# Two input transfers and half a weight transfer, moved to later points of the start

## The reference

```
h    = layernorm(x)                                # per token, over 256 features
x    = x + (gelu_tanh(h @ ctx.T) * (h @ ctx.T)) @ ctx       # ctx: 120 x 256, its own for each batch
h    = layernorm(x)
h    = silu((h @ w1.T) * s1) * ((h @ w2.T) * s2)   # 256 -> 1024, twice
h    = gelu((h @ h1.T) * sh1)                      # 1024 -> 1024
h    = gelu((h @ h2.T) * sh2)                      # 1024 -> 1024
out  = x + (h @ w3.T) * s3                         # 1024 -> 256
```

## Time and profile before

| | us |
|---|---|
| median of 3 executions | 321.84 |
| lowest, highest | 321.80, 322.73 |
| the profiled execution, its own time | 321.71 |
| its span, first to last instruction | 319.9 |
| TensorE busy | 314.5 |
| VectorE busy | 264.6 |
| ScalarE busy | 221.3 |
| GpSimd busy | 58.9 |

### The profile page before, as it was taken

One profiled execution on the slowest core, in us unless ns is written; L12 is line 12 of the kernel. 1 busy time (PEld: TensorE's weight loads), 2 busy tenths in 40 slices (PEclk: granted clock), 3 DMA queues, 4 the chain that ended last, 5 costly groups with the idle time before them and its releaser, 6 DMA issues.

```text
span 319.9 us, 4926 instructions
## 1 busy us (share of the span) xinstructions
PE 314.5 (98%) x1624; PEld 227.1 (71%) x1624; DVE 264.6 (83%) x500; ACT 221.3 (69%) x372; POOL 58.9 (18%) x97
## 2 busy tenths in 40 slices
PE   8899999999999999999999999999999999999996
PEld 5799768775757666577898866886575757666695
DVE  4776996898997899998789585399899998998585
ACT  3657857683887867769924564978678976868760
POOL 4456010411120114114020003000131110201000
PEclk9999999999999999999999999999999999999999
DMA  6799999899999989997518054446699979796003
GB/s 207 252 185 270 207 262 315 320 364 398 316 338 418 310 322 219 340 291 179 154 38 292 3 193 154 180 131 232 228 256 245 420 219 370 152 245 197 2 2 137
DMA packets 31612, 74.89 MB, mean 234 GB/s; under 512 B 2144, under 2 KB 14176, under 8 KB 29024
## 3 DMA queue, kind: packets, MB, share of 16 engines
q0 software_dynamic: 21840, 52.43, 58.3%
q1 hardware_dynamic: 9744, 22.11, 20.4%
HBM read 71.39 MB, written 6.29 MB: 243 GB/s over the span
## 4 chain that ended last, share of the span: by engine, by line
PE 98%; DVE 0%; ACT 0%; issue 0%
PE P L1417 32%; PE P L1411 30%; PE P L1369 19%; PE P L1503 5%; PE P L1490 4%; PE P L1341 2%; PE P L1333 2%; PE P L1322 2%; PE P L1512 1%; PE P L1566 0%; PE P L1579 0%; PE P L1586 0%; PE P L1572 0%; DVE SLY L1172 0%; DVE hh L935 0%
## 5 line engine op out<-in xcount | busy, mean ns | idle before, releaser
L1417 PE MATMUL P<-TL,WR 128*128 128x512 f32 x448 | 107.3, 396 | 0.0
L1411 PE MATMUL P<-TH,WB 128*128 128x512 f16 x448 | 99.8, 379 | 0.0
L1417 PEld LDWEIGHTS P<-TL,WR 128*128 128x128 f32 x448 | 84.0, 188 | 18.5
L671 ACT ACTIVATE TH<-H 128x512 f16<-128x512 f32 x112 | 67.9, 625 | 22.8 <-DVE H L984 14.0
L1411 PEld LDWEIGHTS P<-TH,WB 128*128 128x128 bf16 x448 | 42.4, 98 | 53.1 <-issue 4.5
L991 DVE TENSOR_TENSOR TL<-H,TH 128x512 fp32r<-128x512 f32 x112 | 73.4, 687 | 7.0 <-ACT TH L671 4.5
L1369 PE MATMUL P<-X,W 128*128 128x512 f32 (+1 forms) x320 | 62.4, 351 | 0.0
L1369 PEld LDWEIGHTS P<-X,W 128*128 128x128 f32 x320 | 51.7, 189 | 7.9 <-issue 0.4
L984 DVE TENSOR_TENSOR H<-H 128x512 f32<-128x512 f32 x64 | 41.9, 685 | 0.0
L962 DVE SCALAR_TENSOR_TENSOR H<-P,sc,SLY 128x512 f32<-128x512 f32 (+1 forms) x40 | 25.4, 639 | 18.3 <-PE P L1369 11.0
L692 ACT ACTIVATE H<-P 128x512 f32<-128x512 f32 x48 | 28.5, 593 | 13.7 <-DMA blocks_h<-H 5.4
(11 more groups left out here) (93 smaller groups left out, 255.9 us busy)
## 6 DMA issues: line engine op xcount, KB each, us to landing
WR<-blocks_h POOLq DMA_DIRECT2D x16, 1024.0 KB, 6.9
WR<-in_h POOLq DMA_DIRECT2D x11, 1024.0 KB, 9.0
WB<-blocks_h POOLq DMA_DIRECT2D x16, 512.0 KB, 6.0
WB<-in_h POOLq DMA_DIRECT2D x12, 512.0 KB, 7.5
H<-in_h POOLq DMA_DIRECT2D x8, 512.0 KB, 15.2
blocks_h<-H SPq DMA_DIRECT2D x4, 1024.0 KB, 8.6
SLY<-in_h SPq DMA_DIRECT2D x8, 512.0 KB, 5.6
SLY<-in_w SPq DMA_DIRECT2D x6, 512.0 KB, 7.8
```

The source lines that it names most:

```text
L671: eng.activation(TH[:, f % RING, :], operand(c, L, s, kk), ACT.Copy).then_inc(s_hi, 1)
L1411: return eng.matmul(bank(c, L, s, m)[:, :], WB[r % WRING][:, at:at + 128], TH[:, fill(c, L, s, kk) % RING, :], start=(not lower_first and ...
L1417: return eng.matmul(bank(c, L, s, m)[:, :], WR[r % WRING][:, at:at + 128], TL[:, fill(c, L, s, kk) % RING, :], start=(lower_first and s in ...
```

## The change

On SyncE the scales `sc` are now issued ahead of the first wait. The third batch's input is issued behind the wait for the first half of `W12`, the fourth's behind the wait for the second half, with the context of batches 2 and 3 behind it. On GpSimd the second half of `W12` is issued behind a new wait, for the gate of the second batch.

```diff
             eng.dma_start(ct[:, 0, 1, :], ctx_tok[:, 1, :]).then_inc(s_ct[0], 16)
+            eng.dma_start(sc[:, :], cols).then_inc(s_sc, 16)
+
+            eng.wait_ge(s_w12[0], 16)
             load_x(2)
-            eng.dma_start(sc[:, :], cols).then_inc(s_sc, 16)
-
-            eng.wait_ge(s_w12[0], 16)
+            eng.wait_ge(s_w12[1], 16)
             load_x(3)
-            eng.wait_ge(s_w12[1], 16)
             load_cf(1)
             load_ct(1)
@@ gpsimd
             rstd_half(1, 0)
             rstd_half(1, 1)
+
+            eng.wait_ge(s_h, 2)
             load_w12(1)
             rstd(1, 1)
             load_upper_block(0, h1, BLOCK[0])
```

More of the change, by code:

```diff
@@ L400, in _ @@
             eng.dma_start(ct[:, 0, 1, :], ctx_tok[:, 1, :]).then_inc(s_ct[0], 16)
-            load_x(2)
             eng.dma_start(sc[:, :], cols).then_inc(s_sc, 16)
             eng.wait_ge(s_w12[0], 16)
+            load_x(2)
+            eng.wait_ge(s_w12[1], 16)
             load_x(3)
-            eng.wait_ge(s_w12[1], 16)
             load_cf(1)
```

## The result

The changed kernel takes 324.06 us (median of 10, 323.60 to 326.25) against 321.77 (median of 10, 321.47 to 322.73): 1.0076 times, 95% interval 1.0056 to 1.0096. It is 0.8% slower. The forecast was 322.3 with a range to 323.9: the median lies just outside the range, and nearest to the rival of the late context (323.7).

What follows compares the result with a forecast made beforehand. TensorE was taken to bound the kernel, busy 314.5 of 319.9 us. Gain 0, waits at groups 8 and 9 together 0.5, rest 0: 321.71 gives 322.2, or 322.3 as median; range 321.2 to 323.9.

Steps and rivals of the forecast that it cites:

- the rival of the late context: At score(2): context meets the weight blocks and lands at 23.4 to 25.8; middle price 1.4 us, total 323.7, chance 0.20.
- the one on the fourth input and the context: Ahead of score(2): issued from 17.2 to 18.0, taking 3.9 us, they land at 21.1 and 21.5, in time; price 0.
- signs of being wrong: No chain break before 20 us, second half below 5 us, or TensorE idle at score(2) or the stored-sum product.
- The second half of `W12`: At group 8: issued at 11.8, takes 5.4 us, lands at 17.2 against 17.0; TensorE waits 0.2 us.
- The third input: Before stats(0,2): issued at 12.9, lands at 16.6; VectorE idles 1.55 us, TensorE waits 0.5 us at group 9.
- either a rule or chance: First half's late landing at 12.9: by rule it recurs (322.3); by chance it goes (322.0, chance 0.25).
- The first rival: First half of W12 lands at about 10.4, third input costs nothing, group 8 waits 0.2 us: 322.0, chance 0.25.
- The gain: At the first half of W12: landing earlier brings 0, at most 0.04 us, as TensorE comes only at 12.96.
- The stream behind 18 us: Weight blocks pushed by up to 1.8 us, 1.0 us cover at the stored-sum product: price 0, upper end 0.8.
- The fourth input's own statistics: Fourth input issued at 17.2, lands at 21.1 with 3.9 us, needed at 22.73: price 0.

Runs made afterwards that it cites:

- gate 1.2 us later: Changed kernel with GpSimd's wait ahead of the second half moved 1.3 us on, to the end of the second batch's product with its context: 327.16 us, 1.0159.
- SyncE's part alone: Changed kernel without GpSimd's new wait, so the second half of W12 is issued at about 10.1 us again: 322.63 us, 1.0023.
- The gate alone: Kernel before plus only GpSimd's new wait ahead of the second half of W12, SyncE's queue as before: 323.12 us, 1.0044.
- third input at its old place: Changed kernel with the third batch's input issued ahead of all waits on SyncE again: 325.12 us (six runs), 1.0083.
- context early: Changed kernel with the scores' context issued behind the third input, ahead of the wait for the second half of W12: 323.48 us, 1.0071.

## Why the prediction was wrong

**The step that failed** is the one on the fourth input and the context: "with 3.9 us it lands at 21.5, and has 1.7 us to spare. Price 0". The transfers took 5.1 and 7.2 us. The 3.9 us came from a context issued at 15.85, ahead of most of the weight stream; at 18 it runs in the stream. The same two transfers take 2.7 and 3.0 us with the stream held back. The rate was in the rows: 108 KB per us for a SyncE transfer in that stream, which I used for the rival and not for the sum. The rival gave 23.4 to 25.8 for the landing, and it was 25.2; its price was 1.4 and came out as 1.2, or 1.45 with the slower matmuls behind the stop. So the mechanism was named and priced, and its chance of 0.20 was too low. The argument set against this rival, that the stream starts slowly and these transfers are first in line, was wrong: the first weight block is issued at 15.76, before the fourth input at 17.62. That the rival's total of 323.7 is near 324.06 is in part luck: the other 0.5 us in it stood for the third input, which cost nothing, and the second half cost 0.65 in its place. Of the signs of being wrong one came true: TensorE idles at `score(2)`.

**The second half of `W12`.** Its transfer took 5.4 us, as taken, and group 8 waited 0.65 instead of 0.2. GpSimd started 0.30 us after the gate, not 0.1 (the "issue" piece at 11.94). The gate itself was 0.21 late, but that moves TensorE as well and adds nothing to the wait. Counted as in the prediction, TensorE would come to group 8 at 13.21 + 8 x 0.502 = 17.23, and the half landed at 17.61: 0.38. The other 0.27 is about what the restart at `score(2)` costs too (0.24); what a restart costs had no term in the sum, and why it costs that is not shown. With a gate 1.2 us later the wait is 1.99, with it taken away 0.

**The third input.** In the sum it bore the 0.5 us, and that was wrong in this kernel: it came at 13.0, in 2.5 us. I let it run beside the second half because I kept the first half at 12.9. But the tail goes with the order on SyncE: in the profiles of the kernel before and four experiments with the third input just ahead of `sc` and the waits, the first half took 7.7 to 8.3 us, in the changed kernel and five others with it held, 5.5 to 6.0. I had taken this tail as either a rule or chance, and it was neither. Whether the third input or the later place of `sc` brings it is not shown. The first rival had the landing right (10.4 against 10.54) and the third input free; its 322.0 failed by the same context. The Trainium skill, "DMA: Bandwidth & Descriptors", section "Latency and other measured facts", calls two of the sixteen engines usually slower for GpSimd's transfers; five traces with the tail and six without show that this alone does not bring it here. Where third input and second half do meet (SyncE's part alone), the price was near the 0.5 worked out, 0.56, but by luck: the input was issued at 10.84 instead of 12.9 and took 5.5 us instead of 3.2 to 4.2. The same page, "Queues, rings and completion order", says that a DMA engine takes turns between the queues packet by packet; the 5.5 us beside the half against 2.5 alone agree with that.

**What held.** The gain was 0 as worked out: 2.3 us off the first half bring nothing, as TensorE comes to it behind the gate and a product. The stream behind 18 us costs nothing: the product from the stored sum follows its group in the changed kernel too, with the same 0.26 us before its weight load. The fourth input's own statistics were not late (landed at 22.7, started on at 23.58). Holding the fourth input and context alone is free (321.74).

**What the parts are worth.** The gate alone: 1.3 us. On top, with SyncE's part, the context behind a late half: 323.12 to 324.06, 0.9 (the two were timed in separate series). SyncE's part alone costs 0.8, by another wait, which the gate takes away.

**Open.** Why executions of one kernel lie 1 to 5 us apart is known only in part. The kernel before has long ones too (321.41 to 324.73 in one series of 23). Two of the long profiles here show something: the half clock behind a wait of 2.0 us (third input at its old place), and a last output store that took 1.2 us more at full clock (SyncE's part alone). In the changed kernel the long executions have a clock of 0.999 to 1.000, so there it is not the clock; what it is, no profile here shows. What starts the first half's tail is open too.

## What to carry to other kernels

A transfer's duration is that of the traffic which it meets: before moving an issue, take the duration from a row at the new time, and if only the rate in a crowd is known, use that one for the sum. An issue that moves further into a crowd is paid more than once: here 1.31 us later in issue was 3.06 us later in landing. Where an engine comes to a transfer behind a chain of its own, a faster transfer is worth nothing, while the slack of what is held back for it is real: here 1.5 us of cover went for a gain of 0. When rows give a rival's place and price as cleanly as those of the forecast, it deserves more than a fifth.

## What the runs showed of the hardware

- A GpSimd transfer of 1,024 KB, issued at 4.8 to 5.2 us, took 5.5 to 6.0 us in six profiles, with the third input held on SyncE, and 7.0 to 8.3 us in six with it ahead. Between 10.00 and 10.50 us the DMA share was 0.00 to 0.10 in four of the six long ones, and 0.37 and 0.50 in the other two, so the late part is not always that of one or two of the 16 engines.
- The 240 KB context took 2.8 us from issue to landing when issued at 11.09 (context early), 3.6 at 15.48 (before), 7.2 at 18.00 (changed) and 9.0 at 19.31 (gate 1.2 us later), and 3.0 at 17.86 with the stream of weight blocks held.
- TensorE's granted clock fell to half after it had waited 1.99, 2.00 and 3.31 us in three kernels (0.50, 0.53 and 0.52 in a window of 2 us behind the wait), and stayed at 1.00 after waits of 1.21, 1.34, 1.41 and 1.70 us. At half clock 28 matmuls lost 1.54 us.
- GpSimd issued a transfer 0.30 us after the VectorE operation that it waited for had ended; its arithmetic started 0.1 us after one.
